# Products that nothing reads, put into chunks 1 to 11 on TensorE, where the feed-forward's steps do not exist yet

## The reference

```
x = x + _L0_conv_ref(_gn(x), ...)
t = _to_tokens(x)
t = t + _L1_attn_ref(_ln_t(t), ...)
t = t + _L1_ffn_ref(_ln_t(t), ...)
x = _from_tokens(t, x)
```

```
h = dA_t * h + dBu_t
y = jnp.einsum('ben,bn->be', h, C_t)
```

## Time and profile before

| | us |
|---|---|
| median of the 3 runs shown | 2523.43 |
| lowest and highest of them | 2519.72, 2525.91 |
| the profiled execution, its own time | 2516.53 |
| its span, first to last instruction | 2514.7 |
| busy: DVE, POOL, ACT, PE | 2456.7, 2419.2, 2316.0, 2097.2 |
| mean granted clock of TensorE | 0.977 of full speed |

### The profile page before, as it was taken

The page is one execution under the profiler, slowest core; times in us unless marked ns, Lnnn a source line. Parts: engine busy times, 40 slices in busy tenths (PEclk is TensorE's granted clock), DMA queues, the critical chain, the costliest instruction groups (busy, mean ns, idle before and its releaser), DMA issues.

```text
span 2514.7 us, 34499 instructions
## 1 busy us (share of the span) xinstructions
PE 2097.2 (83%) x10022; PEld 776.5 (31%) x10022; DVE 2456.7 (98%) x2391; ACT 2316.0 (92%) x3960; POOL 2419.2 (96%) x719
## 2 busy tenths in 40 slices
PE   6687777888888888888888888888888888888878
PEld 3222222323333323323333323323333333333323
DVE  7999999999999999999999999999999999999986
ACT  5777777999999999999999999999999999999977
POOL 4999999999999999999999999999999999999991
PEclk8888999999999999999999999999999999999979
DMA  6555555656656566666566566566566566566542
GB/s 240 191 184 174 191 185 182 203 199 206 208 201 208 203 203 202 208 206 214 197 208 209 197 211 207 196 213 209 191 216 208 188 216 203 181 215 206 175 137 74
DMA packets 171386, 494.51 MB, mean 197 GB/s; under 512 B 23072, under 2 KB 44704, under 8 KB 154240
## 3 DMA queue, kind: packets, MB, share of 16 engines
q1 hardware_dynamic: 171200, 492.30, 58.3%
HBM read 400.33 MB, written 91.88 MB: 196 GB/s over the span
## 4 chain that ended last, share of the span: by engine, by line
DVE 67%; issue 13%; POOL 13%; ACT 4%; PE 3%; DMA 1%; DVEq 0%; POOLq 0%; ACTq 0%; SPq 0%
DVE R L1271 50%; DVE D L1255 10%; POOL R L669 9%; POOL D L648 2%; DVE q L1351 1%; ACT DA L834 1%; DVE G L1296 1%; DVE dl L1281 1%; DVE yv L1292 1%; POOL D L657 1%; PE G L1562 1%; DVE th L1304 1%; PE Y L1643 0%; POOL du L641 0%; DVE G L1330 0%
## 5 line engine op out<-in xcount | busy, mean ns | idle before, releaser
L1271 DVE TENSOR_TENSOR_SCAN R<-DA,R,D 128x512 f32<-128x512 f32 x1344 | 1630.0, 1263 | 1.5 <-ACT DA L834 1.5
L669 POOL TENSOR_TENSOR R<-R,Cs 128x2048 f32<-128x2048 f32 x383 | 1453.4, 3817 | 0.0
L834 ACT ACTIVATE DA<-ds,kept_w 128x512 f32<-128x512 f32 x1536 | 1054.6, 688 | 144.2 <-DVE R L1271 130.6
L648 POOL TENSOR_TENSOR D<-us,Bs 128x2048 f32<-128x2048 f32 x193 | 736.8, 3818 | 9.5 <-DMA us<-lo_d 9.5
L1255 DVE TENSOR_TENSOR D<-us,PB 128x2048 f32<-128x2048 f32 x191 | 358.9, 1879 | 7.0 <-DMA us<-lo_d 7.0
L1639 PE MATMUL Y<-R,kept_w 128*32 128x512 f32 x2048 | 273.8, 628 | 26.3 <-POOL R L669 26.3
L1596 PE MATMUL G<-un,wcv 96*128 96x512 f32 x512 | 251.7, 614 | 29.4 <-ACT h L901 29.4
L1271 DVE TENSOR_TENSOR_SCAN R<-DA,D 128x512 f32<-128x512 f32 x192 | 221.7, 1205 | 2.0 <-ACT DA L834 2.0
L1599 PE MATMUL G<-un,wcv 96*64 96x256 f32 x1024 | 138.1, 391 | 59.3 <-ACT xq L882 57.7
L1562 PE MATMUL G<-st,kept_w 128*64 128x256 f32 (+1 forms) x384 | 110.0, 489 | 63.2 <-ACT st L796 63.2
L1562 PE MATMUL G<-sq,kept_w 96*96 96x512 f32 (+1 forms) x256 | 137.2, 618 | 28.5 <-DVE dl L1281 27.2
(11 more groups left out here) (237 smaller groups left out, 3259.0 us busy)
## 6 DMA issues: line engine op xcount, KB each, us to landing
Bs<-bc_d SPq DMA_DIRECT2D x128, 512.0 KB, 5.3
us<-lo_d SPq DMA_DIRECT2D x64, 1024.0 KB, 6.5
ds<-lo_d SPq DMA_DIRECT2D x64, 1024.0 KB, 8.5
Cs<-bc_d SPq DMA_DIRECT2D x128, 512.0 KB, 4.8
us<-hi_d SPq DMA_DIRECT2D x64, 512.0 KB, 6.9
ds<-hi_d SPq DMA_DIRECT2D x64, 512.0 KB, 5.4
lo_d<-dl SPq DMA_DIRECT2D x64, 256.0 KB, 2.0
lo_d<-du SPq DMA_DIRECT2D x64, 256.0 KB, 2.0
```

The source lines that it names most:

```text
L648: nc.gpsimd.tensor_tensor(shaped(D[:, s % NDBU, :, :], s), low(us, s) if s in LOWS else high(us), of_states(Bs, s), ALU.mult).then_inc(don ...
L669: nc.gpsimd.tensor_tensor(shaped(R[:, s, :, 0:T], s), shaped(R[:, s, :, 1:S], s), of_states(Cs, s), ALU.mult).then_inc(hc_done.sem, 1)
L834: nc.scalar.activation(DA[j % NDA][:, :], ds[:, i, :], ACT.Exp, scale=A[:, j:j + 1]).then_inc(exp_done.sem, 1)
L1271: nc.vector.tensor_tensor_scan(R[:, s, q, 1:S], DA[j % NDA][:, :], D[:, s % NDBU, q, :], before, ALU.mult, ALU.add).then_inc(scanned.sem, 1)
```

## The change

In the iterations where a feed-forward step does not exist, TensorE now does a `spin` in its place: two products of 256 columns for a float32 product of 512 columns, one for each of the smaller steps. Each spin takes over the wait for the bank that the step in its place would have. Iterations 1 to 9 get 15 products each, iteration 10 gets 6 and iteration 11 gets 5: 146 in all. No result of theirs is read, no transfer is added, and no other engine's program is changed.

```
                 if there(g - 1):
                     add_skip(g - 1, 1)
+                if 0 < g < 12:
+                    (freed(post_dve, g - 2, 2) or (place(g - 10) == 0 and freed(fold_ev, g - 10, 1))
+                     or freed(f_ln, g - 11) or freed(dl_done, g))
+                    spin(2, G0, *weights)
...
                 if there(g - 1):
                     sum_states(g - 1, 4)
+                if 0 < g < 12:
+                    spin(2, G0, *weights)
...
                     fold(g - 10, 4, G1)
+                if 0 < g < 12:
+                    spin(1, G0, *weights)
...
                     x_proj(g + 1, G3)
+                if 0 < g < 11:
+                    ((place(g - 10) == 0 and freed(fold_ev, g - 10, 4)) or freed(silued, g + 1))
+                    spin(1, G1, *weights)
...
                     out_proj(g - 1, G1)
+                if 0 < g < 10:
+                    (freed(post_dve, g - 2) or freed(post_act, g - 2, 5) or freed(silued, g + 1, 3))
+                    spin(2, G2, *weights)
                 if inside(g - 10):
                     (freed(post_dve, g - 2) or freed(post_act, g - 2, 5) or freed(silued, g + 1, 3))
                     centre_tokens(g - 10, G2)
+                if 0 < g < 10:
+                    spin(2, G2, *weights)
+                if inside(g - 10):
                     centre_x1(g - 10, G2)
                 if there(g - 1):
                     freed(dl_done, g + 1)
                     variance(g - 1, 0, G3)
+                if 0 < g < 10:
+                    freed(dl_done, g + 1)
+                    spin(2, G0, *weights)
...
                     centre(g - 1, G0)
+                if 0 < g < 10:
+                    (freed(f_q8, g - 10) or freed(post_dve, g - 2) or freed(post_act, g - 2, 5)
+                     or freed(silued, g + 1, 3))
+                    spin(1, G2, *weights)
...
                     z_proj(g + 2, 1, G1, H)
+                if 0 < g < 10:
+                    ((place(g - 9) == 0 and freed(fold_ev, g - 9, 2)) or freed(post_ln, g - 1, 1)
+                     or freed(dl_done, g + 1))
+                    spin(1, G3, *weights)
...
                     conv(g + 2, 0, G3, (0, 1))
+                if 0 < g < 10:
+                    (freed(post_ln, g - 1, 2) or freed(f_h16, g - 10, 1) or freed(f_q8, g - 10)
+                     or freed(post_dve, g - 2) or freed(post_act, g - 2, 5) or freed(silued, g + 1, 3))
+                    spin(1, G2, *weights)
```

## The result

The changed kernel takes 2515.61 us in the median of 7 executions (2514.23 to 2516.35), the kernel before 2523.43 us in 7 executions beside it (2516.97 to 2525.91). The ratio is 0.9973, with a 95% interval of 0.996 to 0.9985: faster by 0.27%. Two things differ, the median and the spread: 2.1 us against 8.9 us. Part of the 7.8 us between these medians is luck of the few executions of the kernel before: over all 119 of its timed executions on record (100 beside the experiments, the 12 of copy_a and these 7) its median is 2520.45 us, and over the 19 of the changed kernel it is 2515.61.

What follows compares the result with a forecast made beforehand. GpSimd's own instructions were taken to set the pace at 37.53 us a chunk, with TensorE's spins hidden: 0 gained, 0 lost on a 2514.7 us span. The profiled 2516.5 plus 6.9 to the median gave 2523.4 us, range 2517 to 2531.

Steps and rivals of the forecast that it cites:

- 0 gained: Sum over all added spins: GpSimd sets the pace without idle time, so 0 gained, 0 lost, 0.0 us.
- a smaller form: The 6.9 us between profiled execution and median are all slow-clock stalls in these chunks and come back: 2516.5 us; 2%.
- rival A: Chunks 1 to 9: raising TensorE's clock from 0.92 gives back 27.0 us, 2496.4 us; faster by over 0.3%: 3%.
- One hand-over in a chunk matters: Iteration start: TensorE's second sum, VectorE's second gate and scan, then GpSimd's line 657; VectorE 1.00 us early.
- Only if the second sum ends more than 1.00 us later does GpSimd stall: Iteration start: VectorE's 1.00 us lead over GpSimd's line 657 absorbs any smaller delay of TensorE's second sum.
- The working for full clock: Iteration with 15 spins: 7.5 us more TensorE work, 34.6 of 37.53 us busy, second sum's start unmoved, cost 0.
- the third place: Third later single spin, after the convolution ending at 142.5 us: waits for ScalarE's logarithm until 143.41, ends at 143.9.
- The products' price: Each added product of 256 columns on TensorE takes 0.50 us at full clock, 1.00 us at half clock.
- Rival B: Iteration start at half clock: second sum 4.1 us late, GpSimd stalls 3.1 us; one or two iterations 10%, three or more 7%.
- A reading of the earlier trace: GpSimd's waits: it waits long only behind the last chunk, 36.8 us at line 699.

Runs made afterwards that it cites:

- copy_a: The kernel before, unchanged, for another trace and 12 more executions: 2520.29 us median (2515.24 to 2526.39).
- gate_later_and_spins: Changed kernel without the four spins ahead of iteration 1's two sums, VectorE's first gate one scan later: 2519.96 us, ratio 1.0007 to the kernel before.
- again: The changed kernel once more, unaltered, beside the kernel before: 2515.7 us against 2519.69, ratio 0.9981.
- head_from_2: The changed kernel without the four spins ahead of the two sums of iteration 1: 2514.41 us against 2520.11 of the kernel before, ratio 0.9982.

## Why the prediction was wrong

It said no change, 2523.4 us within 2517 to 2531; the time is 2515.6.

**The step that failed: "0 gained".** GpSimd paces the kernel; in the profile read, and in those of the changed kernel from chunk 2 to 11, it is never idle. But "0 gained" was read from the one profiled execution at 2516.5 us, and then set on a median that lay 6.9 us higher. The term left out is the stalls of the other executions: copy_a, at 2522.44 us, has 5.66 us of them up to chunk 12. The prediction saw this gap, named stalls from a slow clock as its possible cause ("a smaller form" of rival A, giving 2516.5), and gave it 2%. That was the right case, though not all of the 6.9 us: the median of 3 executions, 2523.4, happens to lie 3 us above the 2520.45 of all 119. The gap between a profile's own time and the median was the best evidence that the profile missed something. Of 112 executions of the kernel before, 90 took more than 2517 us; only the two traces show what such time consists of.

**"One hand-over in a chunk matters" was wrong.** The first gate, behind the sum over quad 3, is a second one. In the profile of before it has no wait at chunk 3, since the slow stretch began behind the convolutions; in copy_a the convolutions lay in it, and the first gate waited up to 1.78 us. The prediction worked the first gate out for the changed kernel only, at full clock, and never for the kernel before with the slow stretch in another place. ScalarE is a third: it waits for the products of lines 1562 and 1660, and VectorE for its `DA` and `rs` (chunks 5, 11 and 12 of copy_a).

**"Only if the second sum ends more than 1.00 us later does GpSimd stall" was wrong too,** since lateness is carried from chunk to chunk. VectorE is busy 37.05 of 37.53 us in chunk 2 and as much in chunks 3 to 6, so it can win back some 0.5 us in a chunk. In copy_a, behind the stall of chunk 2, its lead had come back only a little by chunk 3: the four scans from 157.95 us on take 4.80, so the first ends near 159.15, and line 657 starts at 159.31.

```profile
157.95 4.80 DVE L1271 TENSOR_TENSOR_SCAN R<-DA,R,D 128x512 f32<-128x512 f32 x4
```

That is some 0.15 us of lead, for 1.00 in the first profile. Before the next start of line 657 VectorE lost 0.59 us to a wait for a decay and 1.78 us at the first gate. The gate then starts 3.35 us later against the undelayed start of line 657 than in the first profile: line 657 would have started at 198.83 - 1.94 = 196.89, and the gate is 5.50 us ahead of it, for 158.90 - 150.05 = 8.85. The room it had was the lead of 1.00 us and the second gate's wait of 0.5 us, and 3.35 - 1.5 = 1.85 us is close to the stall measured, 1.94.

**The working for full clock was right.** TensorE is busy 32.8 to 33.9 us in a chunk (34.6 worked out), the clock is at 0.99, the second sum waits for GpSimd as before (0.53 us), and the third place waits 1.13 us for the logarithm. The products' price was set at 0.50 us; two of them take 1.06 us, start to start, 0.53 each.

**Rival B** was right in kind: chunk 1 was named as most exposed, and one of the changed kernel's two traces stalls 0.93 us there (3.1 was the bound). Its mechanism is seen in gate_later_and_spins. It does not occur in chunks 2 to 11 of the changed kernel.

**A reading of the earlier trace rows** was incomplete: GpSimd waits long not only behind the last chunk (36.8 us) but also in the start-up, 26.9 us at line 628 and 9.5 at line 648. Both are nearly the same in the changed kernel (26.9 and 9.8), so nothing hangs on it.

**Rival A, the full 27.0 us,** fell for the reason given: the floor of both kernels is GpSimd's. The Trainium skill's rule (TensorE: Matmul & The Clock Gate, HAM oscillation), that idle gaps bring half speed, agrees with the traces of before: in copy_a the products run at half speed from 173.91 us on, behind idle gaps of 0.93 and 1.32 us. Its price, half of the slow time, does not reach the end of this kernel. The profile with a clock of 0.92 over chunks 1 to 9 has no stall there, and copy_a, with 0.87 over the same chunks, which the prediction's sum would price at 342.04 x 0.13 = 44 us, has 5.66 us up to chunk 12.

**Open:** why the low clock meets the convolutions in one execution and the z projection in another is not shown by any run; nor is what makes line 657's last wait 1.3 us in some executions and 2.8 in others. No run takes away the clock's fall and nothing else, or the wait for ScalarE alone, so how much of the gain goes by each of the ways is open.

## What to carry to other kernels

Before forecasting "no change" from a trace without idle time on the pacing engine, compare the profiled execution's time with the median and the spread: a gap of a few us may be stalls that this trace does not hold. Work each hand-over to the pacing engine out for the kernel before too, with TensorE at half speed at every place of the stage, and ask whether the engine between them can win back in one chunk what it loses in it. Filler products are worth having only where they keep the clock up through the whole stage: a part of them brought little or nothing here, and narrow ones cost some 8 us.

## What the runs showed of the hardware

The mean granted clock of the same kernel varied from 0.963 to 0.980 between 112 executions, and its time with it from 2513.61 to 2531.86 us. A kernel with filler products kept 0.983 to 0.987 (again) or 0.981 to 0.989 (head_from_2), with spreads of 2.4 and 2.3 us. Products of 16 columns with a 128 by 128 weight load in float32 did not keep the clock up (0.963 to 0.973 over the run). In chunk 1 TensorE counted 33.79 us busy of 37.52 at a granted clock of 0.87 with them, and 33.93 of 37.48 at 0.95 with products of 256 columns. The two do not compare as work, since at half clock the same products count as more busy time: the convolutions 3.62 us in copy_a, 1.99 at full clock.
